# A decoder layer with routed experts: late weights asked for early, and routing's one-hots made eight at a time with ScalarE's help

## The reference

```
x = layernorm(x + attention(x))          # 16 heads of 64, causal, softmax(q k^T / 8) v, then a projection
x = layernorm(x + cross_attention(x))    # 16 heads of 16 over 77 context tokens, with a mask
x = layernorm(x + experts(x))            # router: softmax of 8 logits, top 2; each expert 256 -> 1024 -> 256, gelu
```

## Time and profile before

| | |
|---|---|
| median of 3 runs | 1607.26 us |
| profiled execution | 1611.98 us |
| its span on the core | 1610.2 us |
| mean granted clock of TensorE | 0.937 |
| busy: PE, DVE, ACT, POOL | 86%, 77%, 62%, 45% |

### The profile page before, as it was taken

How to read it: one execution, slowest core, us unless ns; L and a number is a source line. 1 busy time by engine, 2 the same in 40 slices (tenths; PEclk the granted TensorE clock), 3 DMA queues, 4 the chain that set the end, 5 groups by cost and what they waited for, 6 DMA issues and landing times. The chain is left out here.

```text
span 1610.2 us, 49636 instructions
## 1 busy us (share of the span) xinstructions
PE 1378.3 (86%) x17623; PEld 1159.9 (72%) x17623; DVE 1243.5 (77%) x3420; ACT 990.6 (62%) x2317; POOL 728.2 (45%) x921
## 2 busy tenths in 40 slices
PE   4699999999999999999999999752699999999940
PEld 3488788788878878878887888641488788888830
DVE  4689999999999998999999899737755555555538
ACT  3667787878878788877878867420144344444426
POOL 2135555554564564565565544411133433343326
PEclk9799999999999999999999999855699999999985
DMA  6536434444443434344344333008411411111135
GB/s 171 141 113 186 124 98 125 117 134 117 123 131 104 127 109 135 114 124 138 97 127 125 100 85 76 8 8 334 193 45 48 144 56 49 45 51 49 47 111 216
DMA packets 138891, 178.79 MB, mean 111 GB/s; under 512 B 78782, under 2 KB 110654, under 8 KB 134176
## 3 DMA queue, kind: packets, MB, share of 16 engines
q1 hardware_dynamic: 127616, 153.71, 31.5%
q0 software_dynamic: 6816, 17.71, 3.6%
q10 hardware_dynamic: 4224, 4.19, 0.7%
HBM read 93.79 MB, written 65.93 MB: 99 GB/s over the span
## 5 line engine op out<-in xcount | busy, mean ns | idle before, releaser
L1553 PE MATMUL ps_e<-xt,wres 128*128 128x128 f16 x3408 | 354.5, 220 | 0.8 <-DVE e_y L1630 0.4
L1553 PEld LDWEIGHTS ps_e<-xt,wres 128*128 x3408 | 288.3, 99 | 72.6 <-issue 1.4
L1609 ACT ACTIVATE act_g<-ps_e,b 128x128 f32<-128x128 f32 x568 | 162.2, 368 | 225.0 <-PE ps_e L1553 116.9
L644 ACT ACTIVATE probs<-st_k,nmax 128x128 f32<-128x128 f32 (+1 forms) x512 | 203.6, 447 | 40.6 <-DVE nmax L839 38.0
L1560 PE MATMUL ps_e<-wres,g_hi 128*128 x568 | 214.5, 379 | 1.0 <-DVE g_lo L1639 1.0
L651 ACT ACTIVATE pt_hi<-ps 128x384 f16<-128x384 f32 x256 | 124.8, 488 | 99.6 <-PE ps L399 97.6
L1512 POOL DMA_INDIRECT z_scr<-e_y,dst_i x71 | 84.1, 1184 | 220.9 <-DVE e_y L1630 220.9
L839 DVE CUSTOM_DVE_ANT_0 st_k<-ps,causal 128x128 f32<-128x128 f32 (+1 forms) x512 | 159.8, 348 | 23.1 <-PE ps L391 23.0
L1103 POOL TENSOR_TENSOR o_st<-o_norm,o_st 128x256 f16<-128x256 f32 x128 | 85.9, 671 | 158.9 <-ACT o_st L659 158.9
L1562 PE MATMUL ps_e<-wres,g_lo 128*128 x568 | 154.8, 273 | 0.0
L1627 DVE SCALAR_TENSOR_TENSOR e_y<-ps_e,b 128x256 f32<-128x256 f32 x71 | 30.1, 424 | 156.9 <-PE ps_e L1562 145.8
(11 more groups left out here) (248 smaller groups left out, 4464.1 us busy)
## 6 DMA issues: line engine op xcount, KB each, us to landing
st_p<-in_moe_w SPq DMA_DIRECT2D x24, 768.0 KB, 5.7
w_scr<-st_p SPq DMA_DIRECT2D x24, 768.0 KB, 4.1
wres<-w_scr SPq DMA_DIRECT2D x18, 1024.0 KB, 21.2
v_scr<-v_tok SPq DMA_DIRECT2D x32, 512.0 KB, 2.6
v_pos<-v_scr SPq DMA_DIRECT2D x32, 512.0 KB, 4.5
k_pair<-k_pair SPq DMA_DIRECT2D x32, 512.0 KB, 4.5
z_scr<-zero SPq DMA_DIRECT2D x32, 256.0 KB, 3.6
wres<-z_scr SPq DMA_DIRECT2D x8, 1024.0 KB, 13.3
```

Of the source, the lines that this page charges most:

```text
L644: nc.scalar.activation(probs[:, g % 2, lo_:up_], masked[:, g % 2, lo_:up_], ACT.Exp, bias=nmax[:, g % 2, q:q + 1], scale=-1.0).then_inc(s_ ...
L1553: last = mm(out, w(c * FF + f * P, b, P), xt[:, t % 2, a, c], start=(m == 0), stop=(m == 5))
L1609: nc.scalar.activation(act_g[:, k % 2, f], ps[:, 3 + 2 * (k % 2) + f // 4, (f % 4) * P:(f % 4 + 1) * P], ACT.Gelu, bias=bias[:, f:f + 1], ...
```

## The change

`other_weights()` is called at s = -3, right behind `first_weights()`, and no longer at s = -1. In routing, `hi_f` and `lo_f` are 16-bit. VectorE compares eight columns n in one instruction, for `hot_hi` without the token's number; ScalarE then multiplies each `hot_hi[:, n]` in place by the token's number, 64 instructions. TensorE waits for VectorE's batch of `hot_lo` and for ScalarE's product.

```
--- before.py
+++ after.py
@@ -315,6 +315,7 @@
                 load_x(0)
                 load_x(1)
                 first_weights()
+                other_weights()
             if 0 <= s - 4 < PIECES:
                 piece_in(s - 4)
@@ -330,8 +331,6 @@
             if has(s + 1):
                 key_double(s + 1)
-            if s == -1:
-                other_weights()
             if has(s - 2):
@@ -1267,10 +1266,11 @@
-    hi_f = sb("r_hi_f", [P, 2 * T], F32)
-    lo_f = sb("r_lo_f", [P, 2 * T], F32)
+    hi_f = sb("r_hi_f", [P, 2 * T], F16)
+    lo_f = sb("r_lo_f", [P, 2 * T], F16)
+    BATCH_N = 8
@@ -1330,6 +1332,10 @@
         nc.scalar.activation(ex[:]..., pr[:]..., ACT.Exp).then_inc(s_exp, 1)
+        act.wait_ge(s_const, 10 + PACK)
+        for n in range(2 * T):
+            act.wait_ge(s_own, n // BATCH_N + 1)
+            nc.scalar.activation(hot_hi[:, n], hot_hi[:, n], ACT.Copy, scale=tokens[:, n % T:n % T + 1]).then_inc(s_hot, 1)
@@ -1343,7 +1349,8 @@
-            pe.wait_ge(s_hot, 2 * n + 2)
+            pe.wait_ge(s_lo_hot, n // BATCH_N + 1)
+            pe.wait_ge(s_hot, n + 1)
@@ -1423,10 +1430,12 @@
-        for n in range(2 * T):
-            t = n % T
-            v.tensor_scalar(hot_hi[:, n], iota_hi1[:], hi_f[:, n:n + 1], tokens[:, t:t + 1], ALU.is_equal, ALU.mult).then_inc(s_hot, 1)
-            v.tensor_scalar(hot_lo[:, n], iota_lo[:], lo_f[:, n:n + 1], None, ALU.is_equal).then_inc(s_hot, 1)
+        for b in range(2 * T // BATCH_N):
+            at = slice(b * BATCH_N, (b + 1) * BATCH_N)
+            v.tensor_tensor(hot_hi[:, at], iota_hi1[:].unsqueeze(1).to_broadcast([P, BATCH_N, SLOT_TILES]),
+                            hi_f[:, at].unsqueeze(2).to_broadcast([P, BATCH_N, SLOT_TILES]), ALU.is_equal).then_inc(s_own, 1)
+            v.tensor_tensor(hot_lo[:, at], iota_lo[:].unsqueeze(1).to_broadcast([P, BATCH_N, P]),
+                            lo_f[:, at].unsqueeze(2).to_broadcast([P, BATCH_N, P]), ALU.is_equal).then_inc(s_lo_hot, 1)
```

More of the change, by code:

```diff
@@ L1291, in routing_block @@
     s_place = sem("r_placed")
+    s_own = sem("r_own_ready")
+    s_lo_hot = sem("r_lo_hot")
     s_w = keep["s_w"]
```

## The result

| | before | after |
|---|---|---|
| median | 1607.26 us (5 runs, 1605.83 to 1607.44) | 1598.94 us (5 runs, 1597.07 to 1600.44) |
| ratio, 95% interval | | 0.9948 (0.9937 to 0.9959) |
| profiled execution | 1611.98 us | 1598.94 us |
| its span, granted clock | 1610.2 us, 0.937 | 1597.2 us, 0.942 |

The change takes 8.3 us off; 10.3 were forecast (1597.0). The two profiled executions differ by 13.0, but the one of before stands 4.7 above its median, so 4.7 of those are not the change's.

The account below looks back on a forecast made before the run. Bounds: ScalarE's wait for late projection weights, with TensorE behind it, and VectorE's one-hots in the serial routing stage. Gains of 3.6 and 6.7 sum to 10.3 us, taking the median from 1607.26 to 1597.0; range 1592.5 to 1602.5.

Parts of the forecast that it names:

- The queue is kept in order; `v_in` at 29.7: Start, SyncE's queue: values wait behind the early weights until 28.0, so `v_in` comes at 29.7, 4.7 us later.
- Keys 3.4 late, between 5.2 and 9.9 us from request to landing: Start: first keys land 3.4 us late, the middle of 2.1 and 4.7; request to landing 5.2 to 9.9 us.
- First three weights not slowed: Start: requests waiting behind the first three weights in the queue slow them by nothing, since it takes requests in order.
- The wait of ScalarE goes, and nothing else becomes late: Start: ScalarE's 6.98 us wait for projection weights goes; its work is ready by 42.3, before TensorE needs it.
- the wait only moves: Rival at the start, chance 0.20: keys land 6.5 us late, the early weights give about 0.4 us; 1600.2.
- part 1: Start, late weights asked for early: 6.98 us of wait removed less 3.4 of later keys, 3.6 us gained.
- The one-hot stage takes 17.0 us: Routing: 64 ScalarE products at 0.247 us bound the stage, 17.0 us against 24.17, 7.1 less.
- The rule on VectorE's rate: Routing: 16-bit compares with one repeated element stay at single rate; double rate would give 0.3 us more.
- the gathers run beside the stream and only add 0.6 us to it, and the biases take 0.4 back: Routing to experts: earlier gathers add 0.6 us to the weights' stream; the last bias then takes back 0.4 of 7.1.
- the weights' stream holds the gathers: Rival before the experts, chance 0.14: gathers wait for the empty queue until 1145.2, part 2 gives 5 us; 1598.7.
- part 2: Routing, the changed one-hots: 7.1 us off the stage less 0.4 for the last bias, 6.7 us gained.
- Rule on the queues: Gathers beside the weights' stream: each DMA engine alternates packets between queues, so gathers are slowed but not held.

Follow-up runs that it names:

- e6: The changed kernel with only the projection weights (2 MB) early, the other late weights asked for behind the keys of tile 0 as before; 1595.22 us, ratio 0.9924.
- e7: The changed kernel with only six of 16 heads of the projection weights early, the rest and the other late weights at s = -1; 1594.44 us, ratio 0.9914.
- e4: The changed kernel with both sets of biases asked for ahead of the expert weights; 1601.38 us, ratio 0.9951.
- e5: The changed kernel with the fallback network's 2 MB of weights asked for behind the first two gathers and awaited before the second tile; 1598.12 us, ratio 0.9937.
- e1: The kernel before with only the late weights moved early, routing unchanged; 1604.7 us, ratio 0.998.
- e0: The kernel before again, unchanged, for a second profile; 1608.12 us, ratio 1.0006.
- e3: The changed kernel again, unchanged; 1599.74 us, ratio 0.9949.
- e10: The changed kernel with six heads' projection weights early, the fallback network's weights asked for behind four gathers and awaited at the eleventh tile; 1591.92 us, ratio 0.9905.
- e2: The kernel before with only the one-hots changed, late weights asked for as before; 1602.53 us, ratio 0.9969.

## Why the prediction was nearly right, and where it failed

- **The queue is kept in order; `v_in` at 29.7.** Right: 30.00. e6 and e7 show the cause, since with less in the queue `v_in` comes at 25.7 and 25.2.
- **Keys 3.4 late, between 5.2 and 9.9 us from request to landing.** The duration was 6.6 us, inside the bounds; the landing, 37.1, came 1.7 before the 38.8 of the forecast. But it was set against one execution of before, whose keys were themselves late: three executions without early weights had first scores at 35.6, 32.3 and 32.1, three with the whole move at 37.2, 37.6 and 38.3 (e4 and e5, which have it too, 37.9 and 36.8). By the means of the threes (33.35 and 37.70) the keys are 4.3 late, not 3.4, and the removed wait is 7.2 (6.98, 7.33, 7.23). The difference is 2.9; e1 measured 3.5 (1.8 to 4.7), I forecast 3.6. The miss in this size is within what the times can tell. TensorE's wait for the keys is 8.51 (8.7 forecast), the second group's transposes come at 43.77 (45.7, counted from the slower execution).
- **First three weights not slowed.** They take 5.6, 7.7 and 9.9 us to landing, where the first profile of before has 5.0, 7.2 and 9.3, but e0, with nothing changed, has 5.2, 7.7 and 9.8. So no slowing beyond the difference between executions is seen.
- **The wait of ScalarE goes, and nothing else becomes late.** Right in after, e1 and e3 to e10. The rival that the wait only moves is out: with it part 1 would give 0.4, and e1's interval begins at 1.8.
- **The one-hot stage takes 17.0 us.** Right: 17.03, with products every 0.246 (0.247 forecast), compares 0.75 and 1.21 (0.75, 1.225), and a last gap on ScalarE's chain. Interpolating by columns between rows of other widths, and not taking a row's mean duration for its rate, gave this; the rows' mean of 344 ns beside one every 246 is the same difference.
- **The rule on VectorE's rate.** The Trainium skill ("Vector Engine (DVE) Microarchitecture Reference", Performance modes) has the compare with one repeated element at the single rate; the trace agrees, 0.75 us for 576 columns in 16 bits, as the 32-bit form took the earlier trace rows.
- **The step that failed: the gathers run beside the stream and only add 0.6 us to it, and the biases take 0.4 back.** From casts to experts the kernel after takes 26.55 us, e2 26.51, before and e0 30.99 and 31.05: 4.5 us gained, not 6.7. The stream's end I had nearly right: from its first request to the landing of the last bias it is 51.8 us, against 50.9 before, 0.9 more. The biases did not hold VectorE, whose first copy starts at 1140.44, 2 us behind their landing. What held was what I had charged with bytes alone: I let the gathers start 7.1 us earlier, inside the stream, and land in time for TensorE to start as far behind the reduction as before. Their first row started 4.3 us behind the issue instead of 2.2, and I had not read that GpSimd's drain at the end of the routing block keeps every engine until both gathers have landed. The rival "the weights' stream holds the gathers" comes nearest to this; it gave part 2 5 us.
- **What bounds a still shorter routing is open.** In the kernel after the last weights land at 1135.06, 48.4 us behind the first request, and no start of the experts can come before them. The start is at 53.0. Whether a shorter routing would still move it was not run; that the gathers of e4 landed before the stream had ended speaks for it.
- **Rule on the queues.** The Trainium skill ("DMA: Bandwidth & Descriptors", Queues, rings and completion order) has an engine alternate between queues packet by packet, by which the gathers would be slowed but not held. The trace of e4 agrees for the time in which the rows move (71 packets of q0 and 70 of q1 in two microseconds). That the first row starts 2 us later beside a full q1 does not follow from it; whether the rows or their descriptors came late is open, as the packets don't show the descriptors.
- **The sum.** Part 1 3.6 forecast and 3.5 measured, part 2 6.7 and 4.5 (trace) to 5.7 (time): 8.0 to 9.2, and 8.3 and 8.5 measured for both. That rival gave 1598.7, and the time is 1598.94; my own forecast was 1.9 off. That the rival comes so near is partly luck: it has the experts 5.1 us earlier, by rows that wait for the empty queue and then take 1.5 us, and part 1 with keys 3.4 us late; measured were 4.5 and 4.3.

## What to carry to other kernels

When a stage in front of a long prefetch is shortened, compute when the prefetch ends, from its start and its bytes, not from where it ended relative to the stage. If it now runs past the stage, the small indirect transfers that follow land later than they did on idle queues: here 2.4 us. Look too at where the blocks of a program end: transfers that GpSimd has asked for just before that point can hold all engines there. When a transfer is asked for early to remove a wait, send only as much of it as the first consumer needs: a quarter of the megabytes (0.79 of 3.2, six heads) removed the same wait, and the first scores behind it came where they had been without the move. And take the anchor of a disputed transfer from more than one execution.

## What the hardware showed that I had not expected

- Two gathers of 0.13 MB each, asked for beside a full queue of 8 and 9 KB rows, had their first row 4.1 to 4.7 us behind the issue in six profiles, against 2.2 in seven with that queue empty or all but empty; in e4 they then moved between its rows.
- GpSimd's drain at the end of the routing block lasted until its gathers had landed (to 1138.80 in the kernel after), and the other engines went on only then; SyncE's transfers did not hold it (in e4 the last weights landed at 1142.79, after the drain had ended at 1141.86).
- The granted clock falls in other places from one execution of the same kernel to the next: e0 had 1.00 from 38.5 to 41.5 us, and the first profile of before, which is 3.3 us behind it there, stood at 0.50 from 42 to 55. The first scores likewise came at 35.6 and 32.3 us. Two profiles can thus stand 5.7 us of span apart (1610.2 and 1604.5) with no edit between them.
- Requests for the 64-partition projection weights kept SyncE for 5.24 us when put behind three full megabytes, and 2.95 us later in the program; with six heads only it was 1.40.
